# Graph convolution's relu kept in its PSUM bank, and the steps of four engines merged in a new sequence

## The chip, the cores and the metric

One Trainium2 chip, one core. The time is device microseconds of one execution. Lower is better. The engines are named as the profile names them: PE (TensorE), DVE (VectorE), ACT (ScalarE), POOL (GpSimd), SP (SyncE, which here only issues DMAs).

## What is computed

128 graphs of 128 nodes with 128 features go through four layers, each followed by a residual add and a layer norm. All 20 inputs are f32.

```
x = layernorm(x + L0(x, adj))    # small graph convolutions on 25 nodes, five groups, fused
x = layernorm(x + L1(x, adj))    # attention, 8 heads, with log(adj + 1e-6) added to the scores
x = layernorm(x + L2(x, adj))    # the graph convolution that the change touches
x = layernorm(x + L3(x, adj))    # gated graph network: 5 layers of a GRU cell
```

The third layer in full:

```
degree = sum(adj, axis=-1);  d = degree ** -0.5
norm_adj = adj * d[:, :, None] * d[:, None, :]
L2 = relu(norm_adj @ (x @ W.T + b))
```

## The kernel before, in words

**Tiling.** Four graphs stand side by side as one tile of 128 x 512 f32, which is exactly one PSUM bank. A group of four is called g (0 or 1), and an iteration `it` has both groups, so there are 16 iterations. PSUM has eight banks: `Q[0..3]` for attention, `M2` for the first and the third layer, and `RT`, `RA`, `RB` for the gated layer.

**Passes.** The four layers of one iteration are far too long a chain to run alone, so a pass n works on several iterations at once. Three threads of steps are interleaved. Thread B holds the first layer of iteration n and the third layer of earlier ones. Thread A is attention. Thread R is the gated layer of iterations n-2 and n-3. There are 19 passes (16 and `LAG` = 3). Passes 5 to 12 are all alike and are called body passes below; 0 to 4 are the head and 13 to 18 the tail.

**Order.** Each engine runs a strictly ordered program. `MERGE` is a table with one string for head, body and tail per engine. Each letter says from which lane (A, B, R, and finer lanes such as M for the row maxima of the scores, P for the products with the adjacency) the next step is taken. Inside a lane the order is fixed, so `MERGE` is what decides how the threads are shuffled. Waits between engines are semaphores.

**The third layer** has these steps. `x2` on DVE normalises the second layer's output to `x2` and makes `dinv`. `l2_agg` multiplies by the adjacency into `M2` (L1242), and ACT copies it to `agg2T` (L712). `l2_t` multiplies by the weights into `M2` again (L1247). Then ACT applies relu with the row scale and writes four pieces of 128 x 128 to the SBUF tile `a_r` (L765). DVE adds `x2` to it (L921, result `y3`) and takes the moments. The next user of `M2` is `adj_t` on PE, the transposes of a new adjacency (L1164), which waits for `a_relu`, the relu's semaphore. ACT's relu waits in its turn for `y3` of the group before, since there is one `a_r` only.

**Steps around it that the prediction names.** At the start of a pass POOL computes a power (`pow`, L581), from which DVE makes `dinv` (L818), `dinv0m` (L821) and `a_row` (L825), for the first layer. DVE's `turn` step makes `h_rem` (L945), which PE's `agg` (L1284, L1285) needs; DVE's `hn` step is L951 (`un`, wanted by PE's `z`). POOL's `un` (L624), `x2d` (L610) and `h_lo` (L620) stand near. At the end of a pass DVE normalises the first layer's result to `x1` (L802, out `x`, in `xin`), after POOL's `ve` and `rs` (L568, L572). PE's first step of the next pass needs `x1`. DVE's `he` and `h_new` are L965 and L969. POOL's `begin` is an `h_lo` (L620) as well, after ACT's `h_hi` (L722).

Of the kernel before, what the change touches and what calls it, by code (L numbers as in the profile page):

```python
# [13 lines left out]
GB = 4  # L14
# [41 lines left out]
    tensor=(("BAABBABBBBBBBAABBBAABAABAABAABBAAABBAAABABABABAAAABABABAAABATAATARAARARIAZZBAATBATBRABRRAIAZZBBATBBATARRARBATI"  # L56
             "BAAZBATAARZARRTAIZZTABRRBRTAIZTBZARRARITABATZZBRRRATBIATZZARRARTBAAIZATZATAARARTARBIATZZARRBATARITZZRABRRTIATZ"
             "ZBRRBARIATBZAZTRBBRATRAIBAABZTZABATARBRRATIAZTZRABRRAITABAZZTARRARTIZBATZBRRRTIABZTAZBRRATRAAAZITZATAARARARTIB"
             "ZTZARRBARTAIZTBZRABRARTAIZTZRBRRABTIAZZTABRBARTABRAABIATZZAATBARRTABRITZAZARRABRTIZAZBTRARRTIABZTZBRRTRITAZZAA"
             "BRATRABRAATIAAZZ"),  # L60
            ("TARARTRATIZZABRRABRITABAZZBTRARRTAIZTZRBRRBIATAZZTBBARRARTABBAAIBAZTAATZARRTRATIBZAAZRRABRTIBZATZRARTARITBZAZB"
             "RRATRIAZTZRRARTBAIAAZBZTAA"),
            ("TARATRARITBZZRRBRTIBZAATZARARRBATIATZZRRRBTIAZZABTRABBATRARIAABZZATBAATRBATBRRTIAZZBRRRAITAAZZATBARRTARITBZAZB"
             "RRTBARITZZARRARTAZAABITZAAATARTRATRIBZZRRARATBIZATZABRRRBTIATZZARRRTIABZTAZARBRABRTABZAABBIAZTAATBRARTARTIBZAZ"
             "BARRRTIBZTAZARRRATIABTZZBRRTRABAIZATZARRTABRAAIATAZTRZRARATIAZTZRBARRATABIZABTZBRRRTIAZTAZBRRRAITBAAZZTRBBRART"
             "ABBAIAZBATBZAATRARRTIATZBZRRBRITAZAATAZRARTRATIZZBARRRATBIZATZRRATBARBAAZAITATAZRATRARIBAZTZABRRARTIBAZZTRBART"
             "ARITZZARRRTAIZTAAZRRRTAZIAAZATAATARRTRIATZZRRRATIBZTAZARRARTAIATZZBRRTARAIZTAZARRTARIAAZATZATRRTRITZZRRRBTIZTZ"
             "BRRRTIZTZRRRTIZZTRRTIRTTZZRRRTITZZRRRTIZZTRRRTIZTZRRRTIZTZRRRIZZTTTRRRIZZTTRRRIZZT")),
    vector=(("CBBCBCBBBBCBBBMMMMPPBPPCBBBBMMBMBMPPPPCRAAAAAMMMMCPPPPBMMMMPCPCPRPCAAARACBRASBCRRMMMMBRRBPPRBPCRCPBCRBRMMBRRMM"
             "SRPSPRPCPRAAAARASRCRSMRSMMPRMSSRSRPSRPRPSBRSMMRMSSCRSRPPMSRPRCPRRSRCAAAARRSCASRSCBMSMRRMMSPBRBRPBPRSPSCRSBSBCR"  # L70
             "SRMBMSCRMRBSMSRPPPRSSPSSSARAASRASCSRARSRSMMMRSPMSPRRSPPSRCRMSBSRMMPRSMSCRSRPCPSRRPRRRSCARAAASRCABRSCSMMRSRMBMS"
             "BPRBRBPSBRPSCRPCSSCRSRMBSMRBRMMSSRPPPRSSPSSSAAASARCRSASRRCRMMMSSPRMSSPRSRPPSRRBSSRMMMMRSSCSRRPCSPRRPPRRRRCARAA"
             "ASSCASS"),
            ("BRCBBSRMMRSBMBPRBRMPSCSRPPCRSSCRSRBMSMBRMRSSRPMPRPSSPSSAASSAARRSCARSRCRSMMSMRMPSSRSRPPPSRRBRMSSMMMPRSSCRSRPPSC"
             "RRPSRSAARRAACSSRRCA"),
            ("BRCBSMRRMBBSMMRRBSCRSCPPRPSPSCRSRBMSBRRMSMSBMRPPSSRPPSSRSASRASAACARRSRCSSMRMMSMSPRPRSPPSRRBRMSSMMMPRSSCSRRCSPP"
             "RRPSRRRACSRAAACRSABRSCSMMRRMBBSMBRRPPSBRSCRSPSPBRSCRCSRMRBMSRMSMPBRPPSSPRSSSSAAAACSRARRSRMMSSMMPRSSCRSRPPSPRRS"
             "BRSMMMRMSSCCRSRPPPSRRPRRSRRAAAARBSCARCCSSBRBSRMBMMBSRBRMPPSBRSCRSSPPRSCRCSMRMRMBSMSPRPRSPSPSRSSSRAASAACARSRCRS"
             "SMMRMMSSRRSPPPPSRRRSMMSBMRMSSPPRSRCSRCRPPRRSAARAARCSRCASRSCSMMRRMMPSRRPCSSRPPCSRSCSMRRMSMRRMPSRSCPRPSSPRSSSSAA"
             "AASRASRRCRSSMMRSSMRSRPMPSPRRPSRSMMRMMSSCRSRPPPSRRPRRRSRAAAASRASRSCSRRSRRSRSRSSRSRSRRSSRCSRSSSRRSSSSRSRSSRRSSRR"  # L80
             "SRSRSSRSRSRSSRSSSSSSSSSSSSSSSS")),
    scalar=(("BBBBBBDAAMMMDMAMMMMBBAABAABBMMMMBACMCMMMDRARARARARMRMCMRCRMDRARRMBMRMRMBSRABSARASRASRMSSRMBRMSBMSRRSBRASCRMSCR"
             "MSMRSRMDSARRASRASRARSMMSRCRMSMRCRSSADRSRSMRMSMRSBRSMBRASBSARSRSASARBSMRSMRMBMSRRSASBMRSCRSCRMSMDRSRMSARRARSASR"
             "ARSMRSCRMSMMRCRDSSARSRSRMMSMRBSMRSBARSASBRRASSASRMBMRSMSRMSBRRSBASRSCMRSCRSMSRMRMSDARRASRS"),
            ("ARARSSMRRMCMSCMRDSRSARSSRRMSMBMRSRSMBRABSARSASSRASRMMSRMSBRBMSRSRBASRMRSCMSCRMSMRSRSDASRSARR"),
            ("ARASRMSRCMRSCRMDMRSSRASRSRSMRMSSMBRMRABSRASRBASSARBSRSMSMRMBMSRSRBASRMRSCMSCRSDMSRRMSARSSARARRASRSMMRMRCSMRCSR"
             "SDRSARSRSMRMMRSSMBRABSBASARRSSARSMMRBSMSBRMSRSRSBARSCRMSCMRSMMRSRSDARARRRSSRAASRMSRMCMSMRCSDRSRSASRRMSMMRBSMRS"
             "BRABSASRRASSASBRRSBMSRMMSMRSRBASRMSRSCMRMSCRSRMSDARASRRASRASRMMRCSRMCSMRDSSRARSMSRRMSMRMSRSRASARSASSRASRSRSMRM"
             "SMRSMRSRACSRMSCMRSMMRSRSARSARSRRRSSRRSCRSRSRSCRSRSRSSRRSSSRRSRSRSRSRSRSRRSSRSRSRSSSSSSSSSSSSSS")),
# [1291 lines left out]
```

## Time and profile before

| | |
|---|---|
| time, median of 3 runs | 1654.97 us (1654.43 to 1656.23) |
| the profiled execution | 1655.95 us, of which the span of instructions is 1654.2 us |
| PE busy | 1564.2 us, 95% of the span |
| DVE busy | 1420.3 us, 86% |
| ACT busy | 1237.4 us, 75% |
| POOL busy | 877.1 us, 53% |
| DMA | 25 GB/s mean, 8.4% of the queues' time in the main queue |
| mean granted TensorE clock | 0.991 of full |

Times are in microseconds. A row of the timeline gives the start, the duration, engine, line and operation, then "out<-in" by tile names, and in brackets how long the engine had been idle and who released it. "x4" means four instructions shown as one row. Matmuls are pipelined, so their shown durations overlap.

### The profile page before, as it was taken

The numbers are of one execution on the slowest core, as the hardware profiler recorded it, in microseconds if no ns is written. First come the engines' busy times: TensorE is split into PE (matmuls) and PEld (weight loads), VectorE is DVE, ScalarE is ACT, GpSimd is POOL, SyncE is SP. The second block draws the span as 40 slices with busy tenths as digits, with TensorE's granted clock in tenths as the row PEclk, the third lists the DMA queues.
The fourth block names the chain that finished last, engine by engine and source line by source line (L and its number), as shares of the span: only waits on it lengthen the run. The fifth ranks groups of instructions, "written<-read, shape, count | busy, mean of one in ns | idle before, by whom it ended". The sixth has DMA issues, their size and how long they took to land.

```text
span 1654.2 us, 34075 instructions
## 1 busy us (share of the span) xinstructions
PE 1564.2 (95%) x12166; PEld 1260.4 (76%) x12166; DVE 1420.3 (86%) x3696; ACT 1237.4 (75%) x3015; POOL 877.1 (53%) x1006
## 2 busy tenths in 40 slices
...
GB/s 95 20 43 1 31 27 31 14 13 43 14 31 27 19 26 14 43 14 31 14 27 30 14 31 26 28 18 14 43 14 31 27 18 26 14 27 14 14 1 20
DMA packets 80960, 40.85 MB, mean 25 GB/s; under 512 B 6917, under 2 KB 80794, under 8 KB 80794
## 3 DMA queue, kind: packets, MB, share of 16 engines
...
q14 instruction: 68, 0.56, 0.1%
q10 hardware_dynamic: 396, 0.15, 0.0%
...
## 4 chain that ended last, share of the span: by engine, by line
PE 68%; DVE 16%; ACT 8%; POOL 5%; issue 3%; DMA 0%; SPq 0%; POOLq 0%; DVEq 0%; ACTq 0%
PE RA L1090 16%; PE RB L1090 15%; PE Q L1050 7%; PE RT L1050 4%; PE Q L1201 3%; PE Q L1218 3%; DVE stats L784 2%; ACT e_s L702 2%; PE RT L1284 2%; PE M L1242 2%; PE M L1129 1%; POOL rs L572 1%; PE Q L1184 1%; PE RT L1285 1%; PE M L1050 1%
## 5 line engine op out<-in xcount | busy, mean ns | idle before, releaser
L702 ACT ACTIVATE e_s<-Q,s_ng 128x128 f32<-128x128 f32 x1024 | 293.3, 396 | 33.4 <-DVE s_ng L890 33.2
L620 POOL TENSOR_TENSOR h_lo<-hT,h_hi 128x512 fp32r<-128x512 f32 (+1 forms) x163 | 204.9, 1258 | 166.5 <-ACT h_hi L728 141.2
L628 POOL TENSOR_TENSOR hd<-hT,nn 128x512 f32<-128x512 f32 x156 | 201.6, 1293 | 134.7 <-ACT nn L742 134.2
L624 POOL TENSOR_SCALAR un<-tr 128x512 f32<-128x512 f32 (+1 forms) x164 | 105.3, 643 | 293.6 <-ACT tr L738 293.2
L890 DVE TENSOR_REDUCE s_ng<-Q 128x4 f32<-128x512 f32 x256 | 167.9, 680 | 10.7 <-PE Q L1201 10.7
L899 DVE TENSOR_TENSOR p_s<-Q,adjTe 128x512 f32<-128x512 f32 x256 | 169.2, 680 | 6.4 <-PE Q L1050 4.4
L1050 PE MATMUL Q<-ident,e_s 128*128 128x128 f32 x1024 | 154.3, 276 | 7.6 <-ACT e_s L702 7.3
L742 ACT ACTIVATE nn<-tr,wT 128x512 f32<-128x512 f32 (+1 forms) x164 | 119.0, 728 | 50.7 <-DVE tr L956 49.9
L738 ACT ACTIVATE tr<-RA,b_rz 128x512 f32<-128x512 f32 (+1 forms) x160 | 111.6, 697 | 60.5 <-PE RA L1090 58.8
L1090 PE MATMUL RA<-agg_hi,comp_hi 128*128 128x512 f32 (+1 forms) x320 | 143.8, 449 | 9.0 <-DVE agg_lo L941 8.5
L1050 PEld LDWEIGHTS Q<-ident,e_s 128*128 128x128 f32 x1024 | 123.6, 142 | 34.9 <-ACT e_s L702 14.9
L1090 PE MATMUL RB<-h_hi,whh_hi 128*128 128x512 f32 (+1 forms) x320 | 146.7, 459 | 2.5 <-DVE un L951 2.5
L572 POOL TENSOR_TENSOR rs<-ve,half_neg 128x4 f32<-128x4 f32 x128 | 139.1, 1087 | 10.7
L951 DVE SCALAR_TENSOR_TENSOR un<-RB,b_hn,un 128x512 f32<-128x512 f32 (+1 forms) x160 | 117.6, 735 | 23.3 <-POOL un L624 19.5
L941 DVE TENSOR_TENSOR agg_lo<-RT,agg_hi 128x512 fp32r<-128x512 f32 (+1 forms) x159 | 107.3, 675 | 35.3 <-ACT agg_hi L734 34.3
L965 DVE SCALAR_TENSOR_TENSOR hd<-tz,hd 128x512 f32<-128x512 f32 (+1 forms) x164 | 110.4, 675 | 30.5 <-ACT tz L746 18.8
L734 ACT ACTIVATE agg_hi<-RT 128x512 fp32r<-128x512 f32 (+1 forms) x159 | 94.9, 597 | 49.6 <-PE RT L1285 48.1
L1090 PE MATMUL RB<-h_hi,whh_lo 128*128 128x512 f32 (+1 forms) x320 | 126.2, 394 | 0.0
L1090 PE MATMUL RA<-agg_lo,comp_hi 128*128 128x512 f32 (+1 forms) x320 | 126.0, 394 | 0.0
L1090 PE MATMUL RB<-h_lo,whh_hi 128*128 128x512 f32 (+1 forms) x320 | 125.1, 391 | 0.0
L1090 PE MATMUL RA<-agg_hi,comp_lo 128*128 128x512 f32 (+1 forms) x320 | 125.1, 391 | 0.0
L642 ACT ACTIVATE x<-y,nm,rs 128x128 f32<-128x128 f32 x254 | 104.5, 484 | 25.3 <-DVE nm L798 24.1
...
## 6 DMA issues: line engine op xcount, KB each, us to landing
...
```

Source lines behind the costliest of these rows:

```text
L572: return pool.tensor_tensor(r[:, :], v[:, :], half_neg[:, 0, 0:GB], ALU.pow)
L620: pool.tensor_tensor(h_lo[g][:, c], hT[g][:, c], h_hi[g][:, c], ALU.subtract).then_inc(SG["h_lo"][g], 1)
L628: pool.tensor_tensor(hd[g][:, c], hT[g][:, c], nn[g][:, c], ALU.subtract).then_inc(SG["hd"][g], 1)
L702: ins = act.activation(e_s[:, j, c, :], Q[j][:, c * P:(c + 1) * P], ACT.Exp, bias=s_ng[:, j, c:c + 1])
L738: act.activation(tr[g][:, c], A[:, c], ACT.Tanh, bias=b_rz[:, 0:1], scale=0.5).then_inc(SG["r_act"][g], 1)
L742: act.activation(nn[g][:, c], tr[g][:, c], ACT.Tanh, bias=bih[:, 2:3]).then_inc(SG["n_act"][g], 1)
L890: dve.tensor_reduce(s_ng[:, j, :], Q[j][:, :].rearrange("p (c k) -> p c k", c=4), AX_X, ALU.max, negate=True)\
L899: dve.tensor_tensor(p_s[:, j, :, :].rearrange("p (b h) q -> p b h q", b=2), Q[j][:, :].rearrange("p (b h q) -> p b h q", b=2, h=2), adjTe[ ...
L951: dve.scalar_tensor_tensor(un[g][:, c], B[:, c], b_hn[:, 0:1], un[g][:, c], ALU.add, ALU.mult).then_inc(SG["rv"][g], 1)
L965: dve.scalar_tensor_tensor(hd[g][:, c], tz[g][:, c], 1.0, hd[g][:, c], ALU.add, ALU.mult).then_inc(SG["he"][g], 1)
L1050: return pe.transpose(o, i, ident[0:rows, 0:rows])
L1090: ins = pe.matmul(o[:, cs], weights, moving[:, cs], start=start and i == 0, stop=last is not None and i == len(pairs) - 1)
```

## The change

The relu is written back into `M2`, the bank it is read from. `a_r` and ACT's wait for the former `y3` go. DVE adds from `M2`. Because `M2` is now in use until that add is done, the next writer of the bank waits for `y3` and not for `a_relu`, at two places. Lines that are unchanged move up by one to three.

```diff
@@ the tiles
-        a_r = sb("a_r", [P, GB, P])
@@ scalar
                 elif kind == "l2_t":
                     wait(act, "t_mm", it, g + 1)
                     wait(act, "dinv", it, 2 * g + 2)
-                    if it + g > 0:
-                        wait(act, "y3", it + g - 1, 2 - g)
                     for b in range(GB):
-                        ins = act.activation(a_r[:, b, :], M2[:, b * P:(b + 1) * P], ACT.Relu, scale=dinv[g][:, b:b + 1])
+                        ins = act.activation(M2[:, b * P:(b + 1) * P], M2[:, b * P:(b + 1) * P], ACT.Relu, scale=dinv[g][:, b:b + 1])
                     ins.then_inc(S["a_relu"], 1)
@@ vector
-                    dve.tensor_tensor(cols(y3[g]), cols(a_r), cols(x2[g]), ALU.add).then_inc(S["y3"], 1)
+                    dve.tensor_tensor(cols(y3[g]), M2[:, :], cols(x2[g]), ALU.add).then_inc(S["y3"], 1)
@@ tensor, adj_t
                     elif it:
-                        wait(pe, "a_relu", it - 1, g + 1)
+                        wait(pe, "y3", it - 1, g + 1)
@@ tensor, begin of the last group
-                        wait(pe, "a_relu", it, NG)
+                        wait(pe, "y3", it, NG)
                         keep_warm(10, M2)
@@ MERGE: every string of all four engines is new; the body of POOL as a sample
-            ("BRCSARSRSDRSRSCRSRADSRSASCRASRSRSRSRSRSCDARSDRA"),
+            ("BRSCARSRSCRSRSRSDARSDRSASRSARSCRSRASRCSRSDSRDRA"),
```

In a body pass 61 of PE's 136 steps stand at another place in the row, 56 of DVE's 129, 31 of ACT's 92 and 25 of POOL's 47. Each engine issues the same steps.

**DVE at the start of a body pass.** First before, then after. `dinv` and `dinv0m` are L818 and L821 of before.

```order
L802 TENSOR_SCALAR x<-y_1,mv,rs 128x128 x4
L882 SCALAR_TENSOR_TENSOR dinv<-deg,deg_p 128x4
L885 SCALAR_TENSOR_TENSOR x2d<-deg,deg_p 128x4
L818 SCALAR_TENSOR_TENSOR dinv<-deg,pow 128x10
L821 TENSOR_TENSOR dinv0m<-dinv,member_p 128x10
L945 SCALAR_TENSOR_TENSOR h_rem<-RT,h_tok 128x512
L951 SCALAR_TENSOR_TENSOR un<-RB,b_hn,un 128x512
L890 TENSOR_REDUCE s_ng<-Q 128x4 x2
L956 TENSOR_TENSOR tr<-RA,un 128x512
L941 TENSOR_TENSOR agg_lo<-RT,agg_hi 128x512
L825 TENSOR_TENSOR a_row<-a_i,dinv0m 128x320
```

After:

```order
L799 TENSOR_SCALAR x<-y_1,mv,rs 128x128 x4
L879 SCALAR_TENSOR_TENSOR dinv<-deg,deg_p 128x4
L882 SCALAR_TENSOR_TENSOR x2d<-deg,deg_p 128x4
L815 SCALAR_TENSOR_TENSOR dinv<-deg,pow 128x10
L818 TENSOR_TENSOR dinv0m<-dinv,member_p 128x10
L822 TENSOR_TENSOR a_row<-a_i,dinv0m 128x320
L948 SCALAR_TENSOR_TENSOR un<-RB,b_hn,un 128x512
L942 SCALAR_TENSOR_TENSOR h_rem<-RT,h_tok 128x512
L887 TENSOR_REDUCE s_ng<-Q 128x4
L953 TENSOR_TENSOR tr<-RA,un 128x512
```

`a_row` moved in front of both gated steps, and `un` in front of `h_rem`.

**POOL at the same place**, before:

```order
L581 TENSOR_TENSOR pow<-deg_s,half_neg 128x10
L624 TENSOR_SCALAR un<-tr 128x512
L610 TENSOR_TENSOR x2d<-x,dinv 128x4x127
L620 TENSOR_TENSOR h_lo<-hT,h_hi 128x512
L596 TENSOR_SCALAR adjTe<-adjT 128x512
```

After:

```order
L580 TENSOR_TENSOR pow<-deg_s,half_neg 128x10
L623 TENSOR_SCALAR un<-tr 128x512
L619 TENSOR_TENSOR h_lo<-hT,h_hi 128x512
L609 TENSOR_TENSOR x2d<-x,dinv 128x4x127
L595 TENSOR_SCALAR adjTe<-adjT 128x512
```

`h_lo` and `x2d` changed places.

**PE at the same place** (the scores of attention are `Q<-km,qT`, `agg` is `RT<-a_half`), before:

```order
L1090 MATMUL RB<-h_hi,whh_lo 128x512
L1201 MATMUL Q<-km,qT 128x256 x8
L1284 MATMUL RT<-a_half,h_tok 128x128
L1285 MATMUL RT<-a_half,h_rem 128x128
```

After:

```order
L1198 MATMUL Q<-km,qT 128x256 x8
L1087 MATMUL RA<-agg_hi,comp_hi 128x512
L1087 MATMUL RA<-agg_hi,comp_lo 128x512
L1087 MATMUL RA<-agg_lo,comp_hi 128x512
L1087 MATMUL RB<-h_hi,whh_hi 128x512
L1087 MATMUL RB<-h_lo,whh_hi 128x512
L1087 MATMUL RB<-h_hi,whh_lo 128x512
L1281 MATMUL RT<-a_half,h_tok 128x128
```

Two gate steps (`in` and `z`, three matmuls each) now stand between the scores and `agg`.

## Rows read from the trace of the kernel before

**Rows 1.** Window of seven body passes: us, busy PE, PEld, DVE, ACT, POOL, clock, DMA

```profile
475.07:1167.47 692.40, 665.05 (x5209) 539.95 (x5209) 613.74 (x1584) 538.16 (x1310) 383.07 (x428) 0.99 0.09 24
```

**Rows 2.** Timeline of PE around the border of passes 9 and 10

```profile
870.55 0.66 PE L1050 MATMUL RT<-ident,x 128*128 128x128 f32 x4 [1.42 <-ACT x L642]
...
872.33 1.16 PE L1234 MATMUL Q<-wT,on_ts 128*128 128x128 f32 x8 [0.69 <-ACT on_ts L709]
...
875.68 0.66 PE L1050 MATMUL Q<-ident,x 128*128 128x128 f32 x4 [1.30 <-DVE x L802]
...
883.92 0.22 PE L1284 MATMUL RT<-a_half,h_tok 128*128 128x128 f16 x1 [1.13 <-DVE h_rem L945]
```

**Rows 3.** Timeline of DVE at the start of pass 10

```profile
881.58 0.58 DVE L818 SCALAR_TENSOR_TENSOR dinv<-deg,pow 128x10 f32<-128x10 f32 x1 [1.25 <-POOL pow L581]
882.20 0.98 DVE L821 TENSOR_TENSOR dinv0m<-dinv,member_p 128x10 f32<-128x10 f32 x1
883.10 0.68 DVE L945 SCALAR_TENSOR_TENSOR h_rem<-RT,h_tok 128x512 f16<-128x512 f32 x1
```

**Rows 4.** Timeline of POOL and of ACT at the same place

```profile
881.52 0.63 POOL L624 TENSOR_SCALAR un<-tr 128x512 f32<-128x512 f32 x1
882.12 1.04 POOL L610 TENSOR_TENSOR x2d<-x,dinv 128x508 f32<-128x508 f32 x1
...
881.69 0.63 ACT L728 ACTIVATE h_hi<-hT 128x512 fp32r<-128x512 f32 x1
```

**Rows 5.** L821 and L825 in all 16 iterations, min/median/max ns; L821 in pass 11

```profile
L821 DVE TENSOR_TENSOR dinv0m<-dinv,member_p x16: 136/249/982, 9.4 to 1374.7; 128x10 f32<-128x10 f32 x16
...
L825 DVE TENSOR_TENSOR a_row<-a_i,dinv0m x16: 471/480/702, 9.6 to 1379.5; 128x320 f32<-128x320 f32 x16
...
981.10 0.54 DVE L821 TENSOR_TENSOR dinv0m<-dinv,member_p 128x10 f32<-128x10 f32 x1
```

**Rows 6.** Timeline of DVE and of PE further on in pass 10

```profile
892.32 0.67 DVE L921 TENSOR_TENSOR y<-a_r,x 128x512 f32<-128x512 f32 x1
...
895.27 1.28 DVE L899 TENSOR_TENSOR p_s<-Q,adjTe 128x512 f32<-128x512 f32 x2
...
892.84 0.60 PE L1050 MATMUL M<-ident,adjn 128*128 128x128 f32 x4
...
896.84 1.08 PE L1218 MATMUL Q<-p_s,vp 128*32 128x128 f32 x32
```

**Rows 7.** Timeline of DVE at the end of pass 9

```profile
867.64 0.76 DVE L926 TENSOR_SCALAR a_half<-adjr 128x512 f16<-128x512 f32 x1
...
871.18 0.69 DVE L965 SCALAR_TENSOR_TENSOR hd<-tz,hd 128x512 f32<-128x512 f32 x1
871.90 0.69 DVE L969 SCALAR_TENSOR_TENSOR hT<-hd,nn 128x512 f32<-128x512 f32 x1
...
873.49 2.13 DVE L802 TENSOR_SCALAR x<-xin,mv,rs 128x128 f32<-128x128 f32 x4 [0.83 <-POOL rs L572]
```

**Rows 8.** Timeline of POOL at the end of pass 9

```profile
866.83 1.29 POOL L600 TENSOR_TENSOR x1b<-x,bo_row 128x512 f32<-128x512 f32 x1
...
871.34 0.58 POOL L568 TENSOR_SCALAR ve<-mv 128x4 f32<-128x4 f32 x1 [0.49 <-DVE mv L787]
872.00 1.45 POOL L572 TENSOR_TENSOR rs<-ve,half_neg 128x4 f32<-128x4 f32 x1
873.50 1.27 POOL L620 TENSOR_TENSOR h_lo<-hT,h_hi 128x512 fp32r<-128x512 f32 x1
```

**Rows 9.** The relu, its add and an add from PSUM, min/median/max ns

```profile
L765 ACT ACTIVATE a_r<-M,dinv x128: 358/370/554, 83.7 to 1577.2; 128x128 f32<-128x128 f32 x128
...
L921 DVE TENSOR_TENSOR y<-a_r,x x32: 669/682/923, 85.1 to 1584.2; 128x512 f32<-128x512 f32 x32
...
L915 DVE TENSOR_TENSOR y<-Q,x1b x32: 658/691/693, 65.3 to 1557.1; 128x512 f32<-128x512 f32 x32
```

**Rows 10.** A clean normalisation of the same kind as L802 in rows 8

```profile
879.08 1.11 DVE L802 TENSOR_SCALAR x<-y,mv,rs 128x128 f32<-128x128 f32 x4
```

More of the change, by code:

```diff
@@ L55 @@
 MERGE = dict(
[L56 to L89, printed above, removed]
@@ L90 @@
-    gpsimd=(("BDDBDAADAAACCDDRBARCARRDRCDRRARSRAASRSRSRSCRASRCSRDSRDRSACARSBRSRSRSRSDCRSRADSSRASRASRSRSCRSRCSRSDRADRSABRCASR"
-             "SRSDRASRDSRSCSRSARSACARSRSRSSRRSCRDSRDSRA"),
-            ("BRCSARSRSDRSRSCRSRADSRSASCRASRSRSRSRSRSCDARSDRA"),
-            ("BRCSRSARSDRSRSCRSDARSRSASCARSRSRSRSRSARSDCRDSRABARCSRSRSRSRDSRSRACDSSRSARASRSRCSSRRSARDCSRRDASBRCASRSRSRSARSRS"
-             "CDDRSSRAAASRSRCSRSRSRSRSCRDDRSACARSRSRSDARSDRCSRSRSRSASCARSRSRSRSRSCRSARSRARCSRSRSRSRSRSCRSRSSRSRSRSRRSSRSSSSS"
+    tensor=(("BABBABBBABBBBABBABBAAAABAABAABBAAABBAAABABABABAAAABABAABAABATAATARAARARIAZZBABATTBARABRARIAZZBBATBBAATBBARRATR"
+             "AIATZARZAARRAITAZTZBBRRBRTAAIATZZRBRATRAIABTZZBRRARTIZTAZBARRATARBAIATATZAAZRARATIRBTAZZRRARATBIATZZRARBRTIATZ"
+             "RBZRBRAIATBAZTZRBBRATRAIBABAZZTBBATRAARTATRIABZZRARRTAAIBZATZARRARITBZTZBRRRTIAATZAZBRARTBARAIATZATZAARATRARTI"
+             "ZAZRARBARATIBZTZRABRBRTABITZZRRBRATAIBZTZBARARTABRAABIAZTAATZARRARTIBZZTRABRARBITABAZTZRBRRAITAZTZBARRRTIAABZZ"
+             "ATBARRTARAIZATZA"),
+            ("TARARTRAIZTZRBARABRIATZBZATBRARRTIAZTZBRRBARITBAZZTBARRATRABBAAIZABTAAZTARRTRAIZZTBRARARTBIZAZTABRARTARITBZAZB"
+             "RRRTIAAZTZRRARTBAIABAZAZAT"),
+            ("TARATRARITZZBRARBRATZAIBTZRABRARTIATZZRBARBRTBIZAZTRABRARTABBAAIBAZTAAZTARRTARTIBZZRARRBITABATZAZRARTRATIBZAZB"
+             "RRATARITZZRBARTARABAIZTAZAATARRTARITZZBRRRATBIAAZTZBRRBARTIAZTAZRRRATIBZZATBARRBRABTAIBAABZATZATABRARTRAIZTBRZ"
+             "RARBAATIAZTZBRRRATIABZTZBRRARTBIAZATZARRTARAAIBATZATZRRRAIATZATZRRABRITBAZTZARBARRTIBAZTZRARBRTIBAZTAZRRBBAART"
+             "ABBAIABZATZATABRARTARITZBZRRRBTAIZTAAAZRRARTAITZZRBRRATBIZTZRARAARBTBIZAAAZTAAATARRTARBIATZZABRRRTAIBAZZTRBART"
+             "ARITZZRRARATAIZTAZRRTARIAAZATZAATRARTRIATZZRRRATIAZTZRBARATRAIAZTZBARRTRIAZATZARRTAAARIATZAZTRRTRITZZRRBRTIBTZ"
+             "ZRRRTIZTZRRRTIZZTRRTRITZTZRRRTIZTZRRRTIZZTRRRTIZTZRRRITZZTRRRIZZTTTRRRIZZTTRRRIZZT")),
```

25 lines of the change are left out of this document (added).

## The prediction

> **What bounds the kernel now.** I read the busy time by window first, because an average over all 19 passes hides what the steady part does. Seven body passes last 692.40 us, 98.9 us each, and PE is busy for 665.05 us of them, 96% [rows 1]. DVE is busy 89% (613.74 of 692.40), ACT 78%. So PE is the bound, and all that a new order can win there is PE's idle time: 27.35 us over seven passes, 3.9 us a pass. The window begins and ends at the last stall but two of passes 5 and 12.
>
> Next the timeline of PE, for where that idle time is [rows 2]. The reader is to see four stalls and who ends each: 1.42 us before the transpose of x3 (ACT), 0.69 before the output projection (ACT), 1.30 before the transpose of x1 (DVE), and 1.13 before `agg` (DVE's `h_rem`). They sum to 4.54 us, more than the mean of 3.9, since the fourth is not in every pass. The first three are one place, the pass border; the fourth comes 8 us later. Nearly nothing is left between 884 and 958 us.
>
> Then DVE and POOL at the fourth stall. DVE has waited 1.25 us for the power and issues `dinv` at 881.58, just after POOL's `un` at 881.52 [rows 3, 4]. It lasts 0.58 us and ends at 882.16, with `un` (882.15). `dinv0m` starts at 882.20, just after POOL's `x2d` at 882.12; it lasts 0.98 and ends with `x2d` (883.18 and 883.16). This is ten elements a row, and its minimum is 0.136 us [rows 5]. So DVE stood still behind a POOL instruction, and `h_rem`, next on DVE, began at 883.10. In pass 11 the same `dinv0m` took 0.54 [rows 5]. Over the body passes 5 to 12, the timeline has 0.98 four times (passes 7, 8, 10, 12), 0.47 to 0.56 three times and once 0.17.
>
> The Trainium skill (SBUF — State Buffer, Who interferes with whom) states that a DVE instruction with two SBUF inputs and a GpSimd instruction that reads SBUF lock each other out for their whole length, whichever comes first. The two ends that coincide above agree with it.
>
> **The change, part by part.**
>
> *The relu and its add.* ACT's write goes to PSUM. No ACT instruction of before writes there, so I bound it by rows of the same shape: 358 ns at least, 370 in the median, 554 at most [rows 9]. Were each at the minimum, 128 x 12 ns = 1.5 us less on an engine busy 78%; at a longest 554, 184 x 128 = 23.6 us more, or 0.7 us a step, which nothing excludes but no row makes likely. I take 0, hidden in ACT's idle time; if that cover failed, the adds after it would come 0.7 us late, 32 times. The add reads PSUM instead of SBUF: the nearest row is the other residual add, 691 ns against 682 in the median [rows 9], 9 ns x 32 = 0.3 us more. Its maximum is 693 against 923: the present add, two SBUF inputs, is stretched now and then (4 of 32 in the timeline, 0.5 us together). I take -0.3 us in all.
>
> By the skill's rule above, the add from PSUM cannot be locked out; all stretched cases would go, which is the same 0.5 us. The skill (ScalarE: Activation LUTs, Step-by-step: what each stage is for) also calls ScalarE's write to PSUM the faster one, without a figure for it; no row here shows it.
>
> *ACT's wait removed.* It was for the former group's `y3`, half a pass old. No row names it as a releaser. 0 us.
>
> *PE's wait moved to `y3`.* `adj_t` used to start when the relu was done and now waits one add longer, 0.68 us plus the time until DVE comes to it. Behind it on PE stand `z2`, the last turn of attention and `agg`. In pass 10 `adj_t` ran at 892.84 [rows 6], while DVE's add, begun at 892.32, ended at 892.99 [rows 6]: kept in its place it would lose some 0.2 us. The new order puts three matmuls (`z`, 0.7 us) before it. I take 0. For g = 0 several us lie between. Cover gone: 0.7 us a pass.
>
> *DVE and POOL at the pass start.* POOL now runs `h_lo` right after `un`, and `x2d` third. `h_lo` needs ACT's `h_hi`, which ends at 882.32 [rows 4]. So `dinv0m` at 882.20 meets an empty POOL and takes about 0.15 instead of 0.98: 0.82 us saved in the four collided passes. `dinv` still meets `un`. `a_row` (0.48) comes in front, then `un` and `h_rem`: `h_rem` ends at 882.20 + 0.15 + 0.45 + 0.65 + 0.65 = 884.1 instead of 883.78.
>
> *PE at the same place.* After the scores (end 882.8) come `in` and `z`, 0.7 us each (three matmuls at a spacing of 0.235), and only at 884.2 `agg`. So the stall of 1.13 is filled. But the gain has to survive up to where PE next meets DVE. That is `a 0`, which multiplies p_s: PE reached it at 896.84 and the last p_s ended at 896.55 [rows 6]. DVE has no gap between 881.58 and there, and the new order issues the same set in between. So of 1.13 us only DVE's own saving passes, 0.82, and 0.1 of slack: 0.9 us. In the other four passes PE did not stall at `agg`, and I take 0. **Term: 4 x 0.9 = 3.6 us.**
>
> *The pass border.* DVE's chain sets it: moments of xin, POOL's `ve` and `rs`, then x1. DVE's `he` and `h_new` (two SBUF inputs) stood in between; `ve` took 0.58 and `rs` 1.45 against some 0.2 and 1.0 where DVE is quiet, ending at 873.45 [rows 7, 8]. The new order keeps `he` and `h_new` in front of x1. What changes is that POOL's `x1b` is done earlier, so it (866.83 to 868.12 in rows 8) no longer meets `a_half` (0.76 from 867.64 in rows 7, about half of that in the passes where it is alone), and DVE comes to the moments some 0.35 us sooner; `ve`, `he`, `rs`, `h_new` still run one behind another, so I let only 0.1 pass. Then x1: its four parts take 2.13 us against 1.11 clean [rows 7, 10], because `h_lo` started at 873.50, 0.01 us later, and ran to 874.77. In the new order PE's `begin` stands behind the projection. I walk it: on 0.4, z2 0.7, projection 0.9, `begin` 0.4, two ACT copies 1.2; `h_hi` is ready within 0.1 us of where it was, and `h_lo` meets x1 again. PE's three stalls merge into two, same sum. **Term: 8 x 0.1 = 0.8 us.**
>
> Head and tail: the power chain of the first two passes keeps its place on DVE, and the last two passes hardly change. I take 0, with +-2 us.
>
> Sum: 3.6 + 0.8 + 0.3 = 4.7 us. The profiled execution took 1655.95 (span 1654.2, 1.75 outside), so 1651.25 by it. It stands 0.98 above the median of 1654.97, to which the forecast refers: **1650.3 us**, 0.28% faster.
>
> **The rivals.** A measurement of this kernel can tell about 0.2%, 3.3 us: below 1651.7 is faster, above 1658.3 slower.
>
> *A. As forecast*, 1648 to 1653. For it: rows 3 and 4. Chance 0.35.
>
> *B. The border clears too.* If `h_lo` comes after x1, the normalisation falls from 2.13 to 1.11 and PE's 1.30 goes: 8 x 1.0 more, 4.7 + 8 = 12.7, 1642.3. For it: the two started 0.01 us apart, so the order is open. Against: `h_lo` would have to be 1.1 us later. With part of this, or gains in head and tail, 1643 to 1648. Chance 0.15.
>
> *C. Nothing to be measured.* Each filled stall returns at the next meeting of PE with DVE, which has no gap for 15 us there. Then only 0.8 + 0.3 remains, 1653.9; with small new stalls up to 1658. Chance 0.25.
>
> *D. The collision moves to `a_row`: slower.* `h_lo` (1.27 us) is ready at 882.32 + 0.05, and `a_row`, two SBUF inputs, starts at 882.35. If `h_lo` wins, `a_row` waits for its 1.27 us, and behind it on DVE stand `un` and `h_rem`, for which PE's `z` and `agg` wait. A collided pass then loses 1.27 - 0.82 = 0.45, one of the other four 1.2: 1.8 + 4.8 = 6.6, less 1.1, so +5.5 and 1660.5. It decides the sign when `h_lo` wins in more than half of the passes. Against: `a_row`'s maximum so far is 0.70 [rows 5], in other company. The moved wait on `y3` (0.7 a pass, 5.6 us) would give about the same. Chance 0.25.
>
> The Trainium skill's rule on the shared port (same page and section) is what D rests on: the first to start keeps it. By it neither order is safe, and the sum goes by who is first.
>
> **How the numbers follow.** A gives the time. Range: B down to 1643.5, D up to 1661. Faster: A's 0.35 less the tenth that falls above 1651.7 (0.10), B 0.15, and 0.05 for head and tail, 0.45. Same: C 0.25 and A's 0.10, less that 0.05, 0.30. Slower: D 0.25.
>
> **What would show it.** `dinv0m` at 0.15 to 0.2 us in all body passes, and `a_row` at 0.48. No stall of 1.1 us at `agg`. A body pass of 98.3 instead of 98.9 us. x1 at 2.1 us with `h_lo` beside it. Adds L918 (L921 now) all under 0.70. PE idle before `adj_t` for `y3` near zero. Wrong it would be if `a_row` took 1.7, if body passes stayed at 98.9, or if PE showed stalls of a kind not in rows 2: I have walked two places of some 40 that moved, and the others are the largest unknown.

## The result and the profile after

The changed kernel takes 1638.58 us (median of 3 runs, 1636.08 to 1640.4) against 1654.97; the ratio is 0.9898, with a 95% interval of 0.9875 to 0.9921. It is 1.0% or 16.4 us faster; I had forecast 4.7 us and a range that ended at 1643.5. The profiled execution took 1636.08 (span 1634.2), the fastest of the three. One execution of code_only (below) ran slow, 2297.2 us at a mean clock of 0.62; it is in no ratio, and without it that kernel's median is 1661.59 instead of 1661.66.

| | before | after |
|---|---|---|
| PE busy | 1564.2 us, 95% | 1557.9 us, 95% |
| DVE busy | 1420.3 us, 86% | 1411.0 us, 86% |
| ACT busy | 1237.4 us, 75% | 1231.2 us, 75% |
| mean granted clock | 0.991 | 0.998 |

**The body pass.** The windows of after: first all seven passes, as in [rows 1], then two single ones (us, busy PE, PEld, DVE, ACT, POOL, clock, DMA share, GB/s):

```profile
469.73:1153.93 684.20, 665.34 (x5208) 530.67 (x5208) 607.90 (x1583) 535.96 (x1310) 379.65 (x428) 1.00 0.09 24
...
567.58:664.40 96.82, 94.44 (x744) 76.04 (x745) 85.96 (x227) 76.46 (x188) 54.11 (x62) 1.00 0.09 25
...
860.40:958.23 97.83, 95.09 (x745) 75.80 (x745) 87.01 (x227) 76.58 (x188) 54.24 (x62) 1.00 0.09 24
```

The same window of single passes of before:

```profile
870.55:969.85 99.30, 94.36 (x744) 76.54 (x744) 88.09 (x228) 76.87 (x188) 54.70 (x62) 1.00 0.09 24
969.85:1068.24 98.39, 95.83 (x744) 77.93 (x745) 87.19 (x228) 76.85 (x188) 54.75 (x62) 0.98 0.09 24
```

A body pass takes 97.8 us, where before it took 99.2 at full clock; one pass (567.58) took 96.82. Pass 9 is some 0.3 us longer than its neighbours in every trace here and is left out of such figures. The mean of 98.9 on which I worked was a mixture: three of seven passes of before (6, 9 and 11) had a stretch of PE at half clock and took 98.4 to 98.7. PE's idle time in a pass fell from 4.94 to 2.74 us, but the pass shortened by only 1.47. The other 0.73 came back as busy time of the same 744 matmuls; I have not traced which of them are shown longer.

**The places of [rows 2] to [rows 4].** The timeline of PE around the border of passes 9 and 10 of after:

```profile
860.40 0.65 PE L1047 MATMUL Q<-ident,o_ns 128*128 128x128 f32 x4 [0.71 <-DVE o_ns L907]
...
864.12 1.13 PE L1284 MATMUL RT<-a_bin,x 128*128 128x128 f32 x8 [0.78 <-ACT hT L719]
...
866.12 0.66 PE L1047 MATMUL Q<-ident,x 128*128 128x128 f32 x4 [0.87 <-DVE x L799]
...
874.86 0.23 PE L1281 MATMUL RT<-a_half,h_tok 128*128 128x128 f16 x1
...
883.11 0.62 PE L1047 MATMUL M<-ident,adjn 128*128 128x128 f32 x4
```

DVE at the same place, from the border on:

```profile
863.92 2.14 DVE L799 TENSOR_SCALAR x<-xin,mv,rs 128x128 f32<-128x128 f32 x4
...
872.01 0.58 DVE L815 SCALAR_TENSOR_TENSOR dinv<-deg,pow 128x10 f32<-128x10 f32 x1 [1.25 <-POOL pow L580]
872.63 0.17 DVE L818 TENSOR_TENSOR dinv0m<-dinv,member_p 128x10 f32<-128x10 f32 x1
872.83 0.49 DVE L822 TENSOR_TENSOR a_row<-a_i,dinv0m 128x320 f32<-128x320 f32 x1
...
873.90 0.68 DVE L942 SCALAR_TENSOR_TENSOR h_rem<-RT,h_tok 128x512 f16<-128x512 f32 x1
...
882.26 0.69 DVE L918 TENSOR_TENSOR y<-M,x 128x512 f32<-128x512 f32 x1
```

and POOL:

```profile
864.72 1.26 POOL L619 TENSOR_TENSOR h_lo<-hT,h_hi 128x512 fp32r<-128x512 f32 x1 [1.21 <-ACT h_hi L721]
...
872.85 1.63 POOL L619 TENSOR_TENSOR h_lo<-hT,h_hi 128x512 fp32r<-128x512 f32 x1 [0.26 <-ACT h_hi L727]
```

`dinv0m` takes 0.17 (0.98 in [rows 3]), `a_row` 0.49, `agg` starts without a stall behind `in` and `z`, and `adj_t` at 883.11 follows the matmul ahead of it with no gap, though `y3` ended only at 882.95. The border stalls are 0.71, 0.78 and 0.87 instead of 1.42, 0.69 and 1.30. x1 still takes 2.14: POOL's `h_lo` starts 0.80 us behind it, beside the last of its four parts. The second `h_lo` starts 0.02 us behind `a_row` and takes 1.63 instead of 1.26. Over all iterations (min/median/max ns, as [rows 5] and [rows 9]):

```profile
L818 DVE TENSOR_TENSOR dinv0m<-dinv,member_p x16: 158/170/176, 9.3 to 1359.9; 128x10 f32<-128x10 f32 x16
L822 DVE TENSOR_TENSOR a_row<-a_i,dinv0m x16: 480/492/919, 9.5 to 1360.1; 128x320 f32<-128x320 f32 x16
...
L762 ACT ACTIVATE M<-M,dinv x128: 332/349/487, 80.8 to 1561.7; 128x128 f32<-128x128 f32 x128
L918 DVE TENSOR_TENSOR y<-M,x x32: 670/684/693, 82.2 to 1565.8; 128x512 f32<-128x512 f32 x32
```

**Where the time went.** x1 at the end of pass 5 and of pass 12 cuts both runs into three stretches. The first holds the head and body pass 5, the second the body passes 6 to 12, the third the tail. Before:

```profile
478.01 2.13 DVE L802 TENSOR_SCALAR x<-xin,mv,rs 128x128 f32<-128x128 f32 x4 [0.83 <-POOL rs L572]
...
1170.42 2.12 DVE L802 TENSOR_SCALAR x<-xin,mv,rs 128x128 f32<-128x128 f32 x4 [0.83 <-POOL rs L572]
```

After:

```profile
473.25 2.15 DVE L799 TENSOR_SCALAR x<-xin,mv,rs 128x128 f32<-128x128 f32 x4
...
1157.46 2.14 DVE L799 TENSOR_SCALAR x<-xin,mv,rs 128x128 f32<-128x128 f32 x4
```

The first stretch is 4.8 us shorter (0.1 of it in pass 5), the second 8.2 (692.41 to 684.21, seven passes), and from there to the end of the span 7.0 (483.78 to 476.74). That is 20.0 between the two profiled executions, 3.6 more than between the medians. My forecast had 0 for head and tail.

### The profile page after: what moved, and what is told of

It is laid out like the page before. It is cut to its first block, busy times and chain, and to the rows that moved or that the text cites. A ratio compares the mean times of both kernels' runs of the same rounds, so it can differ in the third digit from the quotient of the medians.

```text
span 1634.2 us, 34075 instructions
## 1 busy us (share of the span) xinstructions
PE 1557.9 (95%) x12166; PEld 1248.0 (76%) x12166; DVE 1411.0 (86%) x3696; ACT 1231.2 (75%) x3015; POOL 869.5 (53%) x1006
## 4 chain that ended last, share of the span: by engine, by line
PE 61%; DVE 26%; ACT 6%; POOL 4%; issue 3%; POOLq 0%; DVEq 0%; ACTq 0%
PE RA L1087 14%; PE RB L1087 14%; PE Q L1047 7%; PE RT L1047 3%; PE Q L1198 3%; DVE stats L781 3%; DVE un L948 2%; DVE p_s L896 2%; PE Q L1215 2%; DVE hd L962 2%; DVE tr L953 2%; DVE s_ng L887 2%; PE M L1126 1%; DVE agg_lo L938 1%; PE Q L1181 1%
```

## The experiments

Every kernel was timed in turn with before, in five rounds (three rounds for three_moves, pe_new and dve_pool_new). A time in us is a median; the ratio to before, with its interval, compares better, as the median of before moved between 1655.2 and 1656.9. A "pass" is the distance of x1 at two neighbouring borders within the body, at full clock unless said otherwise.

### The code without the sequence, and the sequence without the code

```diff
 code_only: after, with
-    MERGE of after
+    MERGE of before
```

> The relu written back into M2, its add from M2 and the two waits on y3, with every string of MERGE as before. Theory 1 (the sequence makes the whole difference): the same time as before within 0.1%, 1654 to 1656, body passes at 98.9 us, adds from M2 never over 0.70 us; at most the 0.3 us of my term. Theory 2 (the bank makes a good part of it: a shorter relu, an add that POOL can no longer stretch, no wait of ACT): 1647 to 1651. Rival 3 (the code is dear in the old sequence, where adj_t follows the relu more closely, and only the new sequence makes room for it): 0.2 to 0.7 us a pass more, 1658 to 1666, with idle time of PE before adj_t that DVE's y3 ends.

1661.66 us, ratio 1.003 (1.0018 to 1.0043): slower than before by 4.8 us. That is rival 3's figure; theory 1 had expected no change. A pass takes 99.52 to 99.57. Aligned matmul by matmul with pass 9 to 10 of before, PE runs level up to `adj_t`, and is 0.31 us late from there to the border. Timeline of PE, then of DVE, in code_only:

```profile
897.44 0.60 PE L1047 MATMUL Q<-ident,e_s 128*128 128x128 f32 x4
898.18 0.63 PE L1047 MATMUL M<-ident,adjn 128*128 128x128 f32 x4
```

```profile
897.35 0.68 DVE L918 TENSOR_TENSOR y<-M,x 128x512 f32<-128x512 f32 x1
```

The four transposes of `e_s`, at 897.44, need 0.43 us like others of their kind (897.01 to 897.44), so PE was free at 897.87; `y3` came at 898.03, and `adj_t` began at 898.18. From x1 to x1 the seven passes took 697.05 us against 692.41, 4.6 more: 7 x 0.31 = 2.2 is this wait, and 2.4 is that the three short passes of before (98.4 to 98.7) have no like here: `dinv0m` takes 0.98 in each of the seven passes.

```diff
 order_only, order_again: before, with
-    MERGE of before
+    MERGE of after
```

> The code of before (a_r, ACT's wait for y3, PE's waits on a_relu) with the whole new sequence. The code alone cost 4.8 us in the old sequence (code_only 1661.66 against 1656.87). Theory 1 (the sequence is all; the moved wait on y3 is hidden in it): as after, 1637 to 1640, body passes 97.8 us. Theory 2 (the bank also gives something once its wait is hidden): 1641 to 1645. Theory 3 (the moved wait still costs 0.3 us a pass in the new sequence, 2.4 us, and the sequence gives more than we see): 1634 to 1636.

1642.52, ratio 0.9927 (0.9914 to 0.9941); a pass 97.9.

> After itself, once more, beside order_again on the same chip. 1636 to 1640.5. With order_again it tells whether the relu in M2 is worth anything in the new sequence.

> The code of before with the new sequence, once more (1642.52 in the last call, 3.9 us above the first three runs of after; its body passes were the same, 97.90 against 97.86, and 2.3 of the 3.9 us lay ahead of pass 5). Theory 1 (the code is worth nothing in the new sequence; what differed were stretches of PE at half clock in the head and a stray pass): within 1.5 us of after_again. Theory 2 (the bank gives 3 to 4 us): 1641 to 1643 with after_again at 1637 to 1639.

After_again 1640.25, ratio 0.9902 (0.9887 to 0.9917); order_again 1643.46, ratio 0.9924 (0.9911 to 0.9936). So the sequence makes the gain, with the old code too. The clean passes are alike (97.90 against 97.84), so in the new sequence the wait on `y3` costs nothing, as forecast. In both pairs the new code is 0.2 to 0.3% ahead, some 3 to 4 us, though the intervals of the second pair touch. In the traces of the second pair, order_again lost 3.1 of its 4.9 us at two stretches of half clock in the tail that after_again did not have. Whether the code has a part in those stretches stays open; theory 2 is not excluded. A part of the difference is there to be read. The old add, with two SBUF inputs, is stretched five times in the new sequence, to 1.77 at most and 2.0 us together; in after the add from M2 never takes more than 0.693. In order_only:

```profile
L921 DVE TENSOR_TENSOR y<-a_r,x x32: 679/692/1768, 83.4 to 1571.0; 128x512 f32<-128x512 f32 x32
```

### Head, body and tail by themselves

```diff
 new_head, new_body, new_tail: code_only, with one of the three strings of every engine
-    head | body | tail of before
+    head | body | tail of after
```

> The code of after, with the new strings for the head (passes 0 to 4) only; body and tail as before. The two traces stand 4.8 us apart at the x1 of the border of pass 5 (478.01 against 473.25). Theory 1: 1649.5 to 1651, some 4.5 us less than the old order, all of it before 475 us. Theory 2: less than code_only by 0 to 2, since the head's gain would be the bank's. Rival: the gain of the head is lost again in the first body passes, where DVE sets the border: equal to code_only.

> The code of after, with the new strings for the eight body passes only. The borders of passes 5 and 13 moved apart by 8.2 us more (4.76 to 12.96). Theory 1: 8 x 1.0 = 8 us less than code_only, about 1647, with body passes of 97.8 us, PE idle 2.7 us a pass, dinv0m at 0.17. By my prediction's terms 4.4 us less, 1650.5. Theory 2: about code_only less 2.

> The code of after, with the new strings for the tail (passes 13 to 18) only. From the border of pass 13 to the end the traces moved apart by 6.9 us (12.96 to 19.9), of which 1.3 are PE at half clock at 1632 in the profiled run of before. Theory 1: 5 to 7 us less than code_only, 1648 to 1650. Theory 2, and my prediction's term for the tail (nothing, within 2): 1653 to 1655.

New_head 1656.48, new_body 1649.06, new_tail 1655.63, against 1661.66 for code_only: 5.2, 12.6 and 6.0 us less, each within some 2.5 us by the intervals. The ratios to before are 0.9997, 0.9956 and 0.9994 (each within 0.0013) against 1.003; their differences added up give 0.9887 for all three, and after had 0.9898 (0.9875 to 0.9921) and, run again, 0.9902. So the three parts are independent of each other as far as this can be measured, and theory 2 falls as the main cause. The body's 12.6 holds the cost of the wait on `y3`, up to 2.5 (8 x 0.31). A window of new_body:

```profile
967.07:1064.93 97.86, 95.13 (x744) 75.86 (x744) 87.02 (x227) 76.56 (x188) 54.24 (x61) 1.00 0.09 24
```

Set beside code_only, x1 in the middle of the pass gains 1.62 to 1.65 us in each pass, and the way from there to the border changes by 0.1 at most: the border itself gives nothing, as my term of 0.1 said.

The tail's gain is in part a row of stalls. PE in code_only, all stalls of 0.5 us or more at the ends of passes 13 and 14 and from there up to 1460:

```profile
1272.32 0.66 PE L1047 MATMUL RT<-ident,x 128*128 128x128 f32 x4 [1.16 <-ACT x L641]
...
1275.21 1.16 PE L1231 MATMUL Q<-wT,on_ts 128*128 128x128 f32 x8 [0.69 <-ACT on_ts L708]
...
1368.85 0.66 PE L1047 MATMUL Q<-ident,o_ns 128*128 128x128 f32 x4 [0.88 <-DVE o_ns L907]
...
1375.81 0.47 PE L1087 MATMUL RA<-agg_hi,comp_hi 128*128 128x512 f32 x1 [1.15 <-DVE agg_lo L938]
...
1377.83 0.66 PE L1047 MATMUL Q<-ident,x 128*128 128x128 f32 x4 [1.09 <-DVE x L799]
...
1395.85 0.63 PE L1047 MATMUL M<-ident,adjn 128*128 128x128 f32 x4 [0.61 <-DVE y L918]
```

PE in new_tail, the same:

```profile
1269.44 0.65 PE L1047 MATMUL Q<-ident,o_ns 128*128 128x128 f32 x4 [0.83 <-DVE o_ns L907]
...
1364.08 0.66 PE L1047 MATMUL Q<-ident,o_ns 128*128 128x128 f32 x4 [0.78 <-DVE o_ns L907]
...
1369.17 0.48 PE L1087 MATMUL RA<-h_hi,whh_hi 128*128 128x512 f32 x1 [0.50 <-POOL h_lo L619]
```

5.58 us of stalls against 2.11, one of the six the wait on `y3` (0.61). From x1 at the end of pass 12 to x1 in the middle of pass 15, new_tail takes 241.1 us, and new_body and three_moves, which have the old tail, 244.7 and 244.3. That is about half of the gain. The rest lies in the half pass behind it (48.3 against 50.1) and behind the last x1 (151.9 against 154.7), and I have not taken it apart.

The head's gain gathers between 184 and 380 us. New_head is 5.1 us ahead of code_only at 380, but 1.9 of that it has at 184 already, where new_body and new_tail, with code_only's head, are as early as new_head: this part is code_only's own execution. It leaves some 3 us; I isolated no single cause for it.

All kept traces can be sorted by their strings. X1 at the end of pass 4 comes at 377.3 to 380.6 in the nine with the old head and at 374.0 to 376.6 in the eight with the new one. From x1 of pass 12 to the end of the span it is 482.8 to 485.6 us in the nine with the old tail and 476.6 to 480.4 in the eight with the new one.

### The collision alone

```diff
 pool_swap: before, POOL's body
-    "BRCSARSRSDRS..."
+    "BRSCARSRSDRS..."
```

> Before, with two letters of POOL's body string changed places: h_lo now runs ahead of x2d at the start of each body pass. Nothing else. The term of my prediction: dinv0m 0.17 instead of 0.98, agg's stall 1.13 down to 0.3, 0.8 us for each pass that had the collision, so a body pass of 98.4 and 1652 to 1653.5 (three passes of before were at 98.4 to 98.7 already, in a stretch at half clock). Rival 1: the gain returns at the next meeting of PE with DVE, 1656 to 1657. Rival 2: h_lo now meets a two-input DVE instruction and takes the gain back or more, 1657 to 1662.

1650.59, ratio 0.9969 (0.9958 to 0.9981): 4.7 us from two letters. A pass went from 99.2 to 98.37. The reader sees the stall at `agg` shrink from 1.13 [rows 2] to 0.32 in its timeline of PE, and the window of the pass:

```profile
978.28 0.22 PE L1284 MATMUL RT<-a_half,h_tok 128*128 128x128 f16 x1 [0.32 <-DVE h_rem L945]
```

```profile
968.66:1067.03 98.37, 94.27 (x746) 76.48 (x746) 87.24 (x226) 76.74 (x188) 55.05 (x61) 1.00 0.09 24
```

This is my term in mechanism and in size: 0.83 a pass, expected 0.8. In the traces the four passes of before that had the collision (99.2 to 99.3) fell to between 98.2 and 98.4. The three short ones stayed as they were (98.39, 98.69, 98.39 before; 98.38, 98.67, 98.37 here), and so did pass 5 (99.34; 99.31), in which `dinv0m` took 0.17 already. Seven passes are 3.6 us shorter. Another 1.4 us lies ahead of pass 5, where the two kernels have the same steps in the same order, so the 4.7 (3.1 to 6.9 by its interval) overstates the two letters. Rival C (lost again at the next meeting) falls here. Rival D is not tested by this run, as `a_row` stands late on DVE, as in before.

### What of the body is not the collision

```diff
 two_moves: code_only, POOL's swap as above, and PE's body
-    turn1, t2, adj_t, t3, z, z2, f_t, agg1
+    turn1, t2, t3, z, adj_t, z2, f_t, agg1
 three_moves: the same, and PE's body
+    t2, turn1, z, adj_t, z2, t3, agg1, f_t
```

> Code_only with two moves in the body: on POOL h_lo ahead of x2d, and on PE adj_t of the pass start two places later, behind t3 and z. Nothing else of the new sequence. Body passes of code_only were 99.53 us. My prediction's two mechanisms: 0.83 for the collision (as pool_swap showed, 99.23 to 98.37) and 0.31 for the wait on y3 that z covers: 98.4 us a pass, 9.1 us less in all, 1652.5. If the wait is not covered by the move: 98.7, 1655. If these two were the whole of the body's gain: 97.9, 1648.5.

> Two_moves with one more move on PE: f_t's transposes, the next user of M2 behind adj_t, stand behind agg of the next layer, as in after. In two_moves PE won 0.31 us at adj_t and lost 0.3 again just ahead of f_t, which needs ACT's copy of adjT out of the same bank. If that copy is the cause: 0.3 us a pass less than two_moves (98.9), so 98.5 to 98.6 and 1653.5 to 1655.5. If the 0.3 had another cause: 98.9 and 1657 as two_moves.

Two_moves 1657.33, ratio 1.0009 (1.0 to 1.0018), a pass 98.9; three_moves 1655.32, ratio 0.9995 (0.9986 to 1.0004), a pass 98.78. Neither reaches 98.4. In two_moves, aligned with code_only at x1, PE was 0.95 to 1.0 us ahead behind `adj_t` (0.8 from the collision, and all of 0.31 cured but 0.1), but only 0.66 ahead from `f_t` on, the next user of M2. In three_moves `agg` stands ahead of `f_t`, as in after, and now PE waits there for DVE's `h_rem`, whose place on DVE is the old one. PE in two_moves, then in three_moves:

```profile
994.76 0.63 PE L1047 MATMUL M<-ident,f_t 128*128 128x128 f32 x4
```

```profile
995.55 0.22 PE L1281 MATMUL RT<-a_half,h_tok 128*128 128x128 f16 x1 [0.21 <-DVE h_rem L942]
```

0.1 us of the 0.3 was gained; were ACT's copy of adjT the only cause, all of it would have been.

```diff
 pe_new: code_only, POOL's swap, PE's whole new body string
 dve_pool_new: code_only, the whole new body strings of DVE and POOL
```

> Code_only with the whole new body string of PE, h_lo ahead of x2d on POOL, and the old strings of DVE and ACT. New_body had 97.9 us a pass, code_only 99.53. If the rest of the gain (some 0.6 us a pass beyond the collision and the wait on y3) is PE's own order at the border and ahead of it: 97.9 to 98.1. If the engines' orders only work together: 98.5 or more, and a pass above 99 would say that the new row of PE waits for the old row of DVE.

> Code_only with the new body strings of DVE and POOL, and the old ones of PE and ACT. POOL's part holds the collision, 0.83 us: 98.7 us a pass if the rest lies with PE (the wait on y3 among it, 0.31), 98.2 if the border is DVE's and POOL's doing, and above 99 if the new row of DVE waits for the old row of PE.

Pe_new 1694.17, ratio 1.0225 (1.0209 to 1.024), a pass 102.97; dve_pool_new 1698.11, ratio 1.0246 (1.0229 to 1.0263), a pass 103.7. That is 3.4 and 4.1 us a pass more than code_only, where all four new rows together take 1.7 off. Two stalls of pe_new at its border, where new_body has 0.70 and under 0.4, and code_only 0.69 for the second:

```profile
994.86 0.65 PE L1047 MATMUL Q<-ident,o_ns 128*128 128x128 f32 x4 [1.07 <-DVE o_ns L907]
...
997.48 1.16 PE L1231 MATMUL Q<-wT,on_ts 128*128 128x128 f32 x8 [1.26 <-ACT on_ts L708]
```

So the remaining 0.5 us a pass is not to be had with PE's new row alone, nor with those of DVE and POOL alone. PE's row and DVE's have to fit each other; whether ACT's new row has a part in it was not tested, nor PE, DVE and POOL together. I have not taken it apart further.

### The border, and a kernel that beats both

```diff
 x1_after_gate: after, POOL's h_lo
+                    if kind == "begin" and g == 0 and HEAD - 1 <= it < TAIL - 1:
+                        wait(pool, "x1", it + 1, 1)
 gate_qkv: the same, and PE's body
-    "TARARTRA..."
+    "TAARRTRA..."
```

> After, with one wait added on POOL: in the body, h_lo of begin waits until DVE's x1 is done. At the border DVE's x1 took 2.14 us in seven of eight passes with h_lo beside it and 1.11 in pass 7, and that pass took 96.82 us instead of 97.84. Theory 1 (x1 stretched by h_lo sets the border): x1 at 1.1 everywhere, body passes at 96.8 to 97.0, 7 x 0.9 us less than after, 1631 to 1633. Rival: PE waits for h_lo instead (0.56 in pass 7) and a_row meets the other h_lo (0.92 in pass 7, as rival D of my prediction had it), so the gain is 0.3 a pass or less, 1636 to 1639.

> x1_after_gate with one more move on PE in the body: attention's qkv ahead of r at the start of a pass, since PE waits 0.78 us for h_lo ahead of r. qkv needs ACT's copy of xT, 0.6 us after the transposes. If PE's first wait counts: 0.1 to 0.2 us a pass less, 1631 to 1632. If r, 3 us later, delays the gated chain (tanh, un, hn) so that PE waits there later: 1634 to 1640.

X1_after_gate takes **1632.92 us**, ratio 0.9867 (0.9853 to 0.988): 1.3% below before, and the fastest kernel here. A pass takes 97.0. Its timelines of DVE, POOL and PE:

```profile
960.77 1.11 DVE L801 TENSOR_SCALAR x<-xin,mv,rs 128x128 f32<-128x128 f32 x4
```

```profile
961.96 1.27 POOL L621 TENSOR_TENSOR h_lo<-hT,h_hi 128x512 fp32r<-128x512 f32 x1 [1.60 <-DVE x L801]
```

```profile
963.38 0.47 PE L1089 MATMUL RA<-h_hi,whh_hi 128*128 128x512 f32 x1 [0.78 <-POOL h_lo L621]
```

x1 takes 1.11 instead of 2.14, PE pays 0.78 of waiting for `h_lo` and has lost its 0.87 before the transposes of x1. What is gained is DVE's: the add behind x1 starts 1.03 us behind it and not 2.06, and 0.84 of this reaches the next border. Gate_qkv: 1633.84, ratio 0.9866 (0.9853 to 0.988), a pass 97.15. The wait was not filled: ahead of qkv PE waits 0.96 for ACT's copy `xT`, and r, the gate whose matmuls stood there, comes 2.8 us later.

```diff
 x1_first_gate_begin: x1_after_gate, with DVE's x1 ahead of he and h_new,
-    vector body  "...RCRSSCA"       tensor body  "...ZAZAT"
+    vector body  "...RCRCSSA"       tensor body  "...ZAZTA"
```

> The same wait, and in the body two steps more moved: DVE's x1 in front of he and h_new (rs is ready 0.4 us before x1 starts), and PE's begin in front of the output projection, so that the ACT copy to hT comes 0.6 us sooner and agg's 0.78 us of waiting is filled. Theory 1: PE reaches x1_t 1.2 to 1.5 us sooner than in after, body passes at 96.3 to 96.6, 1627 to 1631. Rival: he and h_new, now behind x1, run beside h_lo (two SBUF inputs each) and delay the next add; no better than the wait alone, or up to 0.5 us a pass worse, 1632 to 1637.

1649.47, ratio 0.9968 (0.9956 to 0.9981), a pass 98.9: far behind even its rival's figure. DVE, POOL, then PE:

```profile
971.92 0.69 DVE L964 SCALAR_TENSOR_TENSOR hd<-tz,hd 128x512 f32<-128x512 f32 x1
972.64 1.64 DVE L968 SCALAR_TENSOR_TENSOR hT<-hd,nn 128x512 f32<-128x512 f32 x1
```

```profile
972.09 1.64 POOL L621 TENSOR_TENSOR h_lo<-hT,h_hi 128x512 fp32r<-128x512 f32 x1 [1.23 <-DVE x L801]
```

```profile
972.07 0.65 PE L1049 MATMUL Q<-ident,x 128*128 128x128 f32 x4 [0.48 <-DVE x L801]
...
973.88 0.47 PE L1089 MATMUL RA<-h_hi,whh_hi 128*128 128x512 f32 x1 [1.16 <-POOL h_lo L621]
...
975.03 2.04 PE L1183 MATMUL Q<-xT,wT 128*128 128x512 f32 x2
```

`he` was running when `h_lo` was released: `h_lo` takes 1.64 where it takes 1.27 elsewhere, and `h_new` behind it 1.64 where it takes 0.69. That is the rival's mechanism, and larger than I had priced it: both stand ahead of the next add on DVE now, which starts 3.31 us behind x1 instead of 1.03, and DVE stays 2.3 us late up to the next x1. PE is late by as much: two waits 1.8 us apart, 0.48 and 1.16, then from 974.5 to 977.5 half clock, with the first matmuls of qkv at 2.04 and 1.53 where after has 1.12 and 1.02. Which of the two sets the pass was not separated. The window of that stretch has a clock of 0.72:

```profile
973.00:979.00 6.00, 5.08 (x14) 2.69 (x15) 5.88 (x20) 2.67 (x5) 3.33 (x6) 0.72 0.32 87
```

## Why the prediction was wrong

The sign was right, the size too small by 11.7 us, and the range ended 5 us above the median (it ended at 1643.5, though rival B's own figure was 1642.3). By the steps:

**The relu and its add** (-0.3) and **the moved wait** (0). In the old sequence together +4.8, in the new one between 0 and -4, of which clean passes show 0.5 and stretched adds that are gone up to 2.0. The mechanism held: in the old place `adj_t` loses 0.31 (I had said some 0.2), and z ahead of it covers that. The adds are all under 0.70. ACT's write to PSUM takes 349 ns where its write to SBUF took 370. That is under the 358 which I had called the least, but I had taken no gain, and the 2.7 us over 128 lie in ACT's idle time. The Trainium skill (ScalarE: Activation LUTs, Step-by-step: what each stage is for) was right that it is the faster one.

**The collision** (4 x 0.9 = 3.6). Right in mechanism and in size: 3.6 in the trace of pool_swap, all of it in the four passes, and nothing in the other four. What I had not asked is why three of those were free of it. PE ran at half clock ahead of it there. In pass 11 POOL's `un` then began 0.11 us behind `dinv` (981.00 against 980.89) and not 0.06 ahead of it [rows 3, 4]. In code_only no pass from 6 to 12 escapes.

**The border** (8 x 0.1). Right in size: 0.0 to 0.1. x1 still met `h_lo`, 2.14 us, as forecast. PE's stalls there did not merge into two of the same sum, though: three are left, of 2.36 us together instead of 3.41, and this gave nothing. Rival B came true in one pass of eight (567.58, x1 in 1.11, pass 96.82, 1.0 less), and x1_after_gate shows B's price of 1.0 a pass to be 0.8.

**Rival D.** In after `a_row` was stretched in two passes, to 0.79 and 0.92, and not to 1.7; the partner was `un`, which in the pass of 0.92 began 0.05 us ahead of it, not `h_lo`. In the other six body passes `a_row` was first, by 0.00 to 0.02 us, and `h_lo` waited. So that D did not come true was luck, and not something I had shown. Dve_pool_new has it once, in pass 10, with `h_lo` 0.01 us ahead: the pass took 105.84 instead of 103.70. Its DVE and POOL:

```profile
908.40 1.60 DVE L822 TENSOR_TENSOR a_row<-a_i,dinv0m 128x320 f32<-128x320 f32 x1
```

```profile
908.39 1.26 POOL L619 TENSOR_TENSOR h_lo<-hT,h_hi 128x512 fp32r<-128x512 f32 x1 [0.24 <-ACT h_hi L727]
```

**The step that failed** is "Head and tail: ... I take 0, with +-2 us". New_head gave 5.2 and new_tail 6.0: 11.2 us, most of the missing 11.7. By the medians of the kept traces it is 3.0 and 6.7. My ground was that single steps keep their places there. But the tail's stalls in the trace of before were there to be read, at each border, and I had counted stalls in one border of the body only. The second failure is 0.5 us a body pass (98.37 in pool_swap, 97.84 in after, 3.7 us in seven passes), which my walk over two places did not find; it comes only with the rows of several engines together. With it the parts add up to some 3 us more than the 11.7, which is what they are uncertain by. What in the head's order gives its 3 to 5 us stays open. "The others are the largest unknown" stood in the text, but the range gave them 2 us.
